# Earlier piece loads, half-piece sums and an unrolled SP program in the deformable-convolution pass of a fused CNN kernel on one Trainium2 core

## What is computed

```python
x = x + L0(group_norm(x))   # binarised grouped 3x3 convolutions with batch norms
x = x + L1(group_norm(x))   # deformable convolution: 8 groups, 9 taps
```

## Time and profile before

| | before |
|---|---|
| median of 3 runs | 3484.58 us (3480.43 to 3488.9) |
| profiled execution | 3470.21 us, its span 3468.4 us |
| granted TensorE clock, mean | 0.93 |
| busy in the span | PE 82%, PEld 66%, DVE 56%, ACT 58%, POOL 54% |
| 16 DMA engines, mean | 169 GB/s; queue of SP 51.2%, queue of ACT 8.2% of their time |

### The profile page before, as it was taken

One profiled execution on the slowest core, in us unless ns is written; L12 is line 12 of the kernel. 1 busy time (PEld: TensorE's weight loads), 2 busy tenths in 40 slices (PEclk: granted clock), 3 DMA queues, 4 the chain that ended last, 5 costly groups with the idle time before them and its releaser, 6 DMA issues. The chain is left out here.

```text
span 3468.4 us, 117020 instructions
## 1 busy us (share of the span) xinstructions
PE 2841.3 (82%) x47624; PEld 2298.9 (66%) x47624; DVE 1938.6 (56%) x2922; ACT 2020.8 (58%) x4321; POOL 1857.6 (54%) x1450
## 2 busy tenths in 40 slices
PE   4888567777279899898989898898989899898993
PEld 2555345555168677777868777776767777776882
DVE  3554412222366667666666766666676666666661
ACT  1222123322177677777767776676767777776870
POOL 0000000000268677777867777686767777785870
PEclk9999878888699999999989999999999999999996
DMA  4555388787346666666666565656566665656552
GB/s 107 147 143 143 82 205 205 197 198 201 104 136 182 184 177 179 185 179 180 178 189 180 174 180 172 186 166 182 164 190 184 175 192 168 181 174 180 169 175 73
DMA packets 477013, 586.79 MB, mean 169 GB/s; under 512 B 175768, under 2 KB 420960, under 8 KB 476512
## 3 DMA queue, kind: packets, MB, share of 16 engines
q1 hardware_dynamic: 358240, 488.14, 51.2%
q10 hardware_dynamic: 118272, 91.76, 8.2%
HBM read 351.92 MB, written 201.14 MB: 159 GB/s over the span
## 5 line engine op out<-in xcount | busy, mean ns | idle before, releaser
L1251 PE MATMUL acc_p<-abuf,vbd 128*32 128x102 f32 (+7 forms) x27648 | 1093.2, 333 | 57.6 <-DMA abuf<-weight_scratch 49.2
L1251 PEld LDWEIGHTS acc_p<-abuf,vbd 128*32 128x32 f32 (+1 forms) x27648 | 906.9, 144 | 243.9 <-DMA abuf<-weight_scratch 59.0
L1088 ACT ACTIVATE dwt<-xp,wts 128x224 f32<-128x224 f32 x2016 | 800.0, 482 | 106.4 <-ACT wst L1111 101.1
L164 PE MATMUL cv<-cin,wb 128*64 128x392 bf16 x6912 | 633.6, 347 | 159.7 <-DMA cin<-sg 159.7
L960 DVE TENSOR_TENSOR pr<-mh_p,ht 128x864 f32<-128x864 f32 x672 | 668.9, 1050 | 23.2
L164 PEld LDWEIGHTS cv<-cin,wb 128*64 128x64 bf16 x6912 | 440.0, 115 | 347.1 <-issue 107.8
L1230 PE MATMUL win_p<-pr,smat 128*128 128x160 f32 x4032 | 611.2, 306 | 8.4 <-POOL pr L1046 8.4
L1043 POOL TENSOR_TENSOR pr<-pr 128x576 f32<-128x576 f32 x224 | 316.7, 1414 | 516.0 <-DVE pr L960 516.0
L1230 PEld LDWEIGHTS win_p<-pr,smat 128*128 128x128 f32 x4032 | 557.1, 191 | 28.7 <-POOL pr L1046 8.8
L1029 POOL TENSOR_TENSOR dwt<-dwt 128x896 f32<-128x896 f32 x224 | 498.9, 2227 | 4.7 <-ACT dwt L1088 4.7
L1172 PE MATMUL om_p<-wts,omin 64*64 64x216 f32 x3584 | 410.1, 372 | 2.4 <-issue 2.4
(11 more groups left out here) (137 smaller groups left out, 2540.3 us busy)
## 6 DMA issues: line engine op xcount, KB each, us to landing
abuf<-weight_scratch SPq DMA_DIRECT2D x1568, 120.0 KB, 2.6
weight_scratch<-wst ACTq DMA_DIRECT2D x224, 400.0 KB, 3.4
xt<-x SPq DMA_DIRECT2D x128, 392.0 KB, 8.6
rows_scratch<-vsb SPq DMA_DIRECT2D x224, 128.0 KB, 2.6
vbd<-rows_scratch SPq DMA_DIRECT2D x896, 32.0 KB, 2.5
cin<-sg SPq DMA_DIRECT2D x128, 203.0 KB, 3.5
x_scratch<-xt SPq DMA_DIRECT2D x64, 392.0 KB, 5.5
y<-x SPq DMA_DIRECT2D x64, 392.0 KB, 3.7
```

The costliest lines, as they stand in the source:

```text
L164: mm = pe.matmul(cv[c][64 * h:64 * h + 64, 0:CN], wb[:, layer, j, k, :], cin[:, u, r:r + CR, k % 3:k % 3 + W], start=(k == 0 and j == 0), ...
L1088: ins = act.activation(dwt[:, j % 2, k, :].rearrange("p (r w) -> p r w", w=W), image[:, r:r + BR, k % 3:k % 3 + W], ACT.Identity, scale=dw ...
L1251: mm = pe.matmul(acc_p[32 * (2 * s + b):32 * (2 * s + b) + 32, 0:TN].rearrange("p (k w) -> p k w", w=W)[:, k0:k1 + 1, x0:x1], vbd[0:K, 1 - ...
```

## The change

Three things change, all in `l1_pass`.

1. **Loads.** At SP's steps 2 and 4 the pieces 2 and 3 of pair i+1 are loaded, at steps 9 and 12 the pieces 0 and 1 of pair i+2. The first two pieces of pair 1 are loaded ahead of the first step. The three operands, their sizes and their buffers stay the same, and so does the place at the end of a step, behind a store where there is one (steps 2 and 9 now have both).
2. **Sums.** `sum_half` works on 392 pixels; eight of them, one at the same place of DVE's steps 0 to 7, take the place of four of 784 pixels at steps 1, 2, 4 and 6.
3. **SP's program** is written out for all 16 pairs; its hardware loop is gone. The other engines keep theirs.

```diff
-        LOAD_AT = (0, 1, 3, 5)
-        SUM_AT = (1, 2, 4, 6)
+        LOAD_AT = {2: (1, 2), 4: (1, 3), 9: (2, 0), 12: (2, 1)}
+        HALVES = 2 * PIECES
...
-                    wait(sp, y_ok, PIECES * q + k - 1)
+                    wait(sp, y_ok, 2 * (PIECES * q + k - 1))
...
-                    if not last and j in LOAD_AT:
-                        load_piece(i + 1, LOAD_AT.index(j))
+                    if j in LOAD_AT:
+                        ahead, k = LOAD_AT[j]
+                        if i + ahead < pairs:
+                            load_piece(i + ahead, k)
...
-                for j in range(NT):
-                    step(0, j, True, False)
-                with sp.Fori(1, pairs - 1) as i:
+                for k in range(2):
+                    load_piece(1, k)
+                for i in range(pairs):
                     for j in range(NT):
-                        step(i, j, False, False)
-                for j in range(NT):
-                    step(pairs - 1, j, False, True)
+                        step(i, j, i == 0, i == pairs - 1)
...
-                def sum_piece(q, k):
-                    at = slice(PIECE * k, PIECE * (k + 1))
-                    yk = y[:, bass.ts(q % 2, 1), at].rearrange("p a f -> p (a f)")
+                def sum_half(q, h):
+                    k, at = h // 2, slice(BNP * h, BNP * (h + 1))
+                    part = slice(BNP * (h % 2), BNP * (h % 2 + 1))
+                    yh = y[:, bass.ts(q % 2, 1), at].rearrange("p a f -> p (a f)")
...
-                        if j in SUM_AT:
-                            sum_piece(i + 1, SUM_AT.index(j))
+                        if j < HALVES:
+                            sum_half(i + 1, j)
```

More of the change, by code:

```diff
@@ L894, in _ @@
             def _(dve):
-                def sum_piece(q, k):
-                    at = slice(PIECE * k, PIECE * (k + 1))
-                    yk = y[:, bass.ts(q % 2, 1), at].rearrange("p a f -> p (a f)")
+                def sum_half(q, h):
+                    k, at = h // 2, slice(BNP * h, BNP * (h + 1))
+                    part = slice(BNP * (h % 2), BNP * (h % 2 + 1))
+                    yh = y[:, bass.ts(q % 2, 1), at].rearrange("p a f -> p (a f)")
                     dve.wait_ge(xl_in[k % 2], 4 * 16 * (PIECES // 2 * q + k // 2 + 1))
-                    dve.scalar_tensor_tensor(out=yk, in0=yk, scalar=ab3[:, 1:2], in1=x3h[:, k % 2, :],
+                    dve.scalar_tensor_tensor(out=yh, in0=yh, scalar=ab3[:, 1:2], in1=x3h[:, k % 2, part],
                                              op0=ALU.add, op1=ALU.add).then_inc(b3_ok, 1)
-                    dve.wait_ge(b3_ok, PIECES * q + k + 1)
-                    dve.scalar_tensor_tensor(out=yk, in0=l2h[:, k % 2, :], scalar=ab3[:, 0:1], in1=yk,
+                    dve.wait_ge(b3_ok, HALVES * q + h + 1)
+                    dve.scalar_tensor_tensor(out=yh, in0=l2h[:, k % 2, part], scalar=ab3[:, 0:1], in1=yh,
                                              op0=ALU.mult, op1=ALU.add).then_inc(y_ok, 1)
-                    dve.wait_ge(y_ok, PIECES * q + k + 1)
+                    dve.wait_ge(y_ok, HALVES * q + h + 1)
                     dve.tensor_copy(spare[:, :], cst[:, 0, 0:1])
-                    for c in range(2):
-                        part = slice(PIECE * k + BNP * c, PIECE * k + BNP * (c + 1))
-                        dve.bn_stats(bn3[:, 2 * k + c, :], y[:, bass.ts(q % 2, 1), part].rearrange("p a f -> p (a f)")).then_inc(bn3_ok, 1)
+                    dve.bn_stats(bn3[:, h, :], yh).then_inc(bn3_ok, 1)
                 def channel_stats(q):
-                    dve.wait_ge(bn3_ok, 2 * PIECES * (q + 1))
+                    dve.wait_ge(bn3_ok, HALVES * (q + 1))
                     dve.tensor_copy(spare[:, :], bn3[:, 0, 0:1])
@@ L993, in step @@
                               near(i, j, 4, first, last), near(i, j, -2, first, last))
-                for k in range(PIECES):
-                    sum_piece(0, k)
+                for h in range(HALVES):
+                    sum_half(0, h)
                 channel_stats(0)
```

## The result

The changed kernel takes a median of 3287.4 us (3276.6 to 3288.9, 4 runs); the kernel before, run beside it, 3483.0 us (3480.4 to 3488.9, 4 runs). The ratio is 0.943, 95% interval 0.941 to 0.945. Beside a later group of runs it took 3280.2 us, ratio 0.944 (0.941 to 0.947). The forecast was 3297 us.

A forecast was written before the change was run, and what follows sets the result against it. PE was taken as the bound in quiet steps, with 20.8 us a pair lost elsewhere. Saving 12.7 us a pair times 14 is 178 us, with first and last pairs together 188: 3484.6 - 188 = 3297 us, range 3225 to 3375.

The forecast's parts named there:

- 132.7 + 7.6 + 0.5 = 140.8 us: L1 pass, one pair: PE's time without waits, plus stalls behind four loads, plus scatter of quiet steps; 153.5 before.
- First and last pair: Outside the 14 pairs: first pair gains 10 us, last gains 1 us at loop's exit, uncovered first half sums cost 0.5.
- The seam: SP between two pairs: the 3.7 us gap at the loop's branch goes, 14 times, and no new one comes.
- Loads' waits to zero: DVE's waits for loaded pieces, with the part of PE's loss they cause, vanish; wait for `l2h` under 20 us in total.
- PE's wait for the weights grows from 45 to about 100 us: PE's wait for `abuf` before `apply`, found in steps 5, 7, 12 and 1, three behind each load.
- 4 loads, 7.6 us: Weight stalls a pair: 2 x 1.6 us for loads alone plus 2 x 2.2 us for loads behind a store.
- the 1.4 us to spare: Weights' trip through HBM in a quiet step: ready at 10.2 us after `windows`, needed by `apply` at 11.6.
- The halves: DVE's half sums: 1.75 us each, 3.25 with the whole's 1.5 us surplus; fit DVE's idling and cover, costed at nothing.
- the cover of 5.5 us: How late DVE can be with `read_misc` and `copy_om` before PE has to wait for them.
- The third rival: DVE's half sums become the bound, each pass held by POOL's long instruction, 6.0 us a half: 3527 us, chance 0.03.
- The first rival: Loads delay nothing that matters or weights arrive in time; pair 133 to 136 us, 3213 us, chance 0.12.
- The second: Each load delays two reads of weights, four stalls of 3.9 us, or pieces still come late: 3412 us, chance 0.15.

The follow-up runs named there:

- experiment 1: The kernel before with only SP's loop written out, loads and sums as they were: 3444.9 us, ratio 0.989.
- experiment 7: The changed kernel with SP's pairs 1 to 13 put back in a hardware loop: 3311.8 us, ratio 0.952.
- experiment 3: The changed kernel with each load moving 8 columns in place of 784 from pair 2 on: 3216.7 us, ratio 0.924.
- experiment 9: The changed kernel with loads at steps 1, 4, 8 and 12, of only 8 columns from the third pair on: 3209.2 us, ratio 0.923.
- experiment 5: The changed kernel with the loads of steps 2 and 9 moved to steps 1 and 8, away from the stores: 3231.5 us, ratio 0.928.
- experiment 6: The changed kernel with each load split over two steps, only one part still at a step with a store: 3226.8 us, ratio 0.927.
- experiment 2: The changed kernel with four whole sums of 784 pixels at steps 1, 2, 4 and 6 again: 3295.0 us, ratio 0.945.

## Why the prediction was right

- **The pair.** Forecast 132.7 + 7.6 + 0.5 = 140.8 us; measured 140.85. Times 14, 178 us forecast and 177.6 measured.
- **First and last pair.** Forecast 10 us for the first and half a us more for the rest; the first gave 16.1 and the last nothing. That is the 6 us by which the profiled execution (3276.55) stands below its 3282. The median stood 14.4 us over the profiled execution before and 11 after.
- **The seam.** Right: 3.7 us became 0.1, nothing took its place, and experiments 1 and 7 price it at 24 to 38 us.
- **Loads' waits to zero, PE's wait for DVE gone.** Right: neither row is left in the waits of the L1 pass beyond 1 us.
- **PE's wait for the weights grows from 45 to about 100 us, behind the loads.** Right in size (106.4, again 101.9 us) and mechanism: with small loads it falls to 49.5 us. The forecast gave the issue beside a store half a us; in 6 of 14 pairs it kept SP from reading at step 3 for 1.3 to 4.8 us, though most of a stall is the late write. The terms of the sum were mis-sized one by one. Store and load together: 2.2 taken, 2.6 and 2.2 measured. A load alone: 1.6 taken, 0.2 (step 7) and 0.6 (step 1) measured. Missing: the 0.9 us at step 4, where ACT is late behind PE's short edge steps, and small waits all over the pair. "4 loads, 7.6 us" was right as a sum by luck: a term too large by 2.4 us met others that were left out. The table's 7.2 us are all the waits ahead of `apply`; the remaining 0.9 us of the 8.1 over 132.7 are longer steps of other kinds, for which the forecast had 0.5. The 1.6 came from one step of the trace, which was taken as the rule; on the mean, a load alone nearly fits into the 1.4 us to spare.
- **The halves.** "Costed at nothing" holds for the time: without them it is 8 to 15 us longer, with intervals that overlap, so they are at best a small gain. The step behind it failed. "A half is 1.6 us, say 1.75", with the surplus 3.25, was to be DVE's load; measured are 3.3 us in nearly every step, so the upper bound was the rule. The median of a half pass in the loop is 1.03 and 1.66 us where half the work would be 0.6. The step of DVE came out at 9.8 us where 10.0 was the bound, and the cover of 5.5 us carried the lag of some 2 us over eight steps. The third rival's mechanism is there in nearly every half, as the last section shows: a pass is held until POOL's instruction is over. But the pass came when part of an instruction of about 1.5 us was over, and did not wait for a whole one of 2.14: the rival needs 5.6 us a half to decide, and found 3.3.
- **The first rival (the loads hide, 3213 us)** describes experiments 3 and 9, where they have no bytes, and comes near 5 and 6, where they keep clear of the stores. **The second (3412 us)** showed only single rows, as the 5.26 us above.

Taken one after the other, the seam is 38 of the 196 us (experiment 1), the loads' new places 150 (experiment 2 against 1) and the halves the last 8, which the noise doesn't part from nothing. Taken out of the kernel after, the seam is 24 to 32. Loads at steps 1 and 8 in place of 2 and 9 bring another 49 to 56 us (experiment 5).

## What to carry to other kernels

Where a small round trip through HBM is on the path, work out its slack once for a quiet step and then ask of each bulk transfer which trip it precedes. Two bulk transfers in one step cost far more than the same two in neighbouring steps, and moving one is a number in a table. And don't halve a vector instruction's cost with its size where POOL works beside it: read the duration of the small form beside POOL, or take the full one.

## What the runs showed that was not expected

- **Traffic adds up steeply.** PE's wait is 0.2 and 0.6 us behind a load of about a megabyte alone and 2.6 and 2.2 us behind that load and a store of 392 KB. The trip has slack, and only what goes over it counts. The same transfers with 8 columns leave 0.7 and 0.3 us, so most of it is bytes, and the rest is SP's issue.
- **Halved instructions kept their length.** 392 columns take 0.61 us alone and 1.03 and 1.66 us (medians) in the loop beside POOL's instructions of 1.4 to 2.4 us. As wholes of 784 columns the two passes have means of 1.48 and 2.02 us:

```profile
L903 DVE SCALAR_TENSOR_TENSOR y<-l2h,ab,y 128x784 f32 (+1 forms) x64 | 129.1, 2017 | 2.3
...
L900 DVE SCALAR_TENSOR_TENSOR y<-y,ab,x3h 128x784 f32 (+1 forms) x64 | 94.8, 1482 | 15.4 <-DMA l2h<-l_scratch 15.1
```

  The columns after the bar are busy us in total and mean ns. The halves need 204.0 + 129.1 = 333 us for what the wholes do in 224. The traces say why. In the kernel after, 239 of the 256 half passes start while an instruction of POOL runs, and each of the 239 ends 0.42 us after that instruction has ended, within 0.01 us; the 17 others, 16 of them before the loop, take 0.61 to 0.63 us. The whole passes of experiment 2 end 0.83 to 0.87 us after POOL's instruction. Those of the kernel before end 0.83 to 1.02 us after it or, with POOL idle, take 1.03 us: in the earlier trace rows the pass of 1911.19 ends at 1912.64, 0.83 us after POOL's instruction beside it, which ends at 1911.81:

```profile
1910.39 1.42 POOL L1043 TENSOR_TENSOR pr<-pr 128x576 f32<-128x576 f32 x1 [11.04 <-DVE pr L960]
```

  So a pass that starts beside POOL is held to the end of POOL's instruction, and only the 0.42 or 0.83 us behind it depend on the columns. A whole piece is held twice, its two halves four times. The Trainium skill ("SBUF — State Buffer", Who interferes with whom) says that a DVE instruction with two SBUF inputs and a GpSimd one that reads SBUF exclude each other; these rows agree. No run here took POOL's work away.
- **The branch of a loop cost 3.1 to 3.4 us on SP and under 0.3 us on DVE, ACT and POOL** in the same program. The loop's length doesn't sort them: a turn has 322 instructions in the trace of SP, 241 in DVE's, 410 in ACT's and 164 in POOL's. Why they differ is open.
